# Splitting the chain of small sums behind the keys and values of a linear attention layer

## The reference, cut to what matters

```
q = x @ Wq[i] + bq[i];  k = x @ Wk[i] + bk[i];  v = x @ Wv[i] + bv[i]
Q = elu(q) + 1;  K = elu(k) + 1
KV   = sum over the rows of K * v          # one number for each of 128 columns
Ksum = sum over the rows of K              # the same
Z = 1 / (Q * Ksum + 1e-6)
V = Q * KV * Z
a = gelu(gelu(V @ Wo[i] + bo[i]))
x = layernorm(a + x);  h = gelu(x @ W1[i] + b1[i]);  f = gelu(h @ W2[i] + b2[i]);  x = layernorm(f + x)
```

## Time and profile before

| | us |
|---|---|
| median of three runs | 479.62 |
| the three runs | 478.72, 479.62, 481.2 |
| the profiled execution, its own time | 478.65 |
| its span in the trace | 476.5 |
| outside the span | 2.15 |

### The profile page before, as it was taken

How to read it: one execution, slowest core, us unless ns; L and a number is a source line. 1 busy time by engine, 2 the same in 40 slices (tenths; PEclk the granted TensorE clock), 3 DMA queues, 4 the chain that set the end, 5 groups by cost and what they waited for, 6 DMA issues and landing times.

```text
span 476.5 us, 6527 instructions
## 1 busy us (share of the span) xinstructions
PE 442.0 (93%) x2074; PEld 309.2 (65%) x2074; DVE 402.6 (85%) x1391; ACT 371.9 (78%) x483; POOL 13.9 (3%) x19
## 2 busy tenths in 40 slices
PE   7697999999999999999999999999989999799992
PEld 6465665756575656566656665667566756688992
DVE  5988889995989698969896988698878897978897
ACT  3989877989897989798889888989888717778106
POOL 0000000000000000000000000000000003230000
PEclk9978999999999999999999999999999999999997
DMA  8200000000100000001000000000010102000003
GB/s 285 70 2 0 22 3 0 1 0 1 45 0 2 23 0 1 1 0 45 0 2 1 1 0 1 0 1 2 0 45 12 34 7 82 2 0 23 2 23 132
DMA packets 5360, 10.40 MB, mean 22 GB/s; under 512 B 848, under 2 KB 1872, under 8 KB 5328
## 3 DMA queue, kind: packets, MB, share of 16 engines
q1 hardware_dynamic: 5040, 9.47, 6.1%
q10 hardware_dynamic: 288, 0.52, 0.3%
HBM read 7.90 MB, written 2.10 MB: 21 GB/s over the span
## 4 chain that ended last, share of the span: by engine, by line
PE 41%; DVE 32%; ACT 19%; issue 7%; DMA 1%; ACTq 0%; SPq 0%; DVEq 0%
PE tile L1249 10%; PE tile L1268 7%; PE tile L1226 6%; PE tile L1222 6%; PE tile L1223 5%; DVE stats L770 5%; ACT y L369 3%; DVE y L911 3%; DVE nt L777 2%; ACT y L374 2%; PE tile L1339 2%; PE tile L1328 2%; ACT aa L388 2%; DVE y L880 2%; ACT kq L348 2%
## 5 line engine op out<-in xcount | busy, mean ns | idle before, releaser
L1249 PE MATMUL tile<-h,w 128*128 128x512 f32 x256 | 113.9, 595 | 0.9 <-ACT h L395 0.7
L1222 PE MATMUL tile<-xh,wh 128*128 128x512 f32 x224 | 97.6, 436 | 6.1 <-DVE xh L793 3.4
L1223 PE MATMUL tile<-xh,wl 128*128 128x512 f32 x224 | 89.2, 398 | 0.0
L1249 PEld LDWEIGHTS tile<-h,w 128*128 128x128 f32 x256 | 47.4, 190 | 54.8 <-issue 51.7
L395 ACT ACTIVATE h<-tile,vec 128x1024 f32<-128x1024 f32 x64 | 71.0, 1117 | 13.1 <-PE tile L1226 12.3
L1226 PE MATMUL tile<-xl,wh 128*128 128x512 f32 x224 | 71.1, 398 | 0.7 <-DVE xl L298 0.3
L403 ACT ACTIVATE nt<-tile,work 128x128 f32<-128x128 f32 x140 | 50.7, 482 | 11.3 <-DVE work L739 11.3
L1222 PEld LDWEIGHTS tile<-xh,wh 128*128 128x128 f32 x224 | 42.6, 190 | 24.9 <-DVE xh L793 5.3
L770 DVE BATCH_NORM_STATS2 stats<-tile 128x6 f32<-128x128 f32 x256 | 52.8, 280 | 0.1
L1226 PEld LDWEIGHTS tile<-xl,wh 128*128 128x128 f32 x224 | 41.6, 188 | 13.5 <-DVE xl L799 2.7
L1223 PEld LDWEIGHTS tile<-xh,wl 128*128 128x128 f32 x224 | 42.8, 191 | 9.1 <-issue 2.2
(11 more groups left out here) (173 smaller groups left out, 669.6 us busy)
## 6 DMA issues: line engine op xcount, KB each, us to landing
x<-x_t SPq DMA_DIRECT2D x7, 512.0 KB, 4.1
out_r<-x SPq DMA_DIRECT2D x8, 256.0 KB, 2.0
raw_u<-layers SPq DMA_DIRECT2D x4, 256.0 KB, 3.2
w<-layers SPq DMA_DIRECT2D x4, 256.0 KB, 3.3
raw_a<-layers SPq DMA_DIRECT2D x4, 192.0 KB, 2.8
x<-x_t ACTq DMA_DIRECT2D x2, 256.0 KB, 3.9
wo<-layers SPq DMA_DIRECT2D x4, 64.0 KB, 4.2
fc<-fc_t SPq DMA_DIRECT2D x1, 256.0 KB, 6.5
```

What stands on the lines that cost most here:

```text
L1222: pe.matmul(dst, wh[:, w0:w0 + P], xh[:, part(n, p, at)], start=True, stop=False)
L1223: pe.matmul(dst, wl[:, w0:w0 + P], xh[:, part(n, p, at)], start=False, stop=False)
L1249: mm = pe.matmul(dst, w2[:, (t - 1) // 2 % 2, j * P:(j + 1) * P], h[:, p, j * PAIR + at:j * PAIR + at + BANK], start=(j == 0), stop=(j == ...
```

## The change

`fold_kv` is replaced by six functions. `key_sum`, `key_limits` and `key_inverse` hold the total of the keys, the scale and the limit, and the reciprocal. They are called right behind the step's second keys, which is ahead of values(t, 0) in steps 2 to 7, ahead of both values in step 0 and ahead of queries(1, 1) in step 1. `value_sum`, `value_ratio` and `folded_weights` stay at the place of fold_kv. The scale is now the second increment of `folded` instead of the third, and share_log waits for that.

```
 def share_log(t, p):
-    act.wait_ge(folded, t * FOLD_STEPS + 3)
+    act.wait_ge(folded, t * FOLD_STEPS + 2)
...
-def fold_kv(t):
-    for p in range(2):
-        dve.wait_ge(kv_ready[p], t + 1)
-    dve.wait_ge(wo_in[q], 16 * (t // 4 + 1))
-    dve.tensor_tensor(col[0], ksum[:, 0:1], ksum[:, 1:2], ALU.add).then_inc(folded, 1)
-    dve.tensor_tensor(col[1], kvsum[:, 0:1], kvsum[:, 1:2], ALU.add).then_inc(folded, 1)
...
+def key_sum(t):
+    for p in range(2):
+        dve.wait_ge(k_ready[p], t + 1)
+    dve.tensor_tensor(fold_col(0), ksum[:, 0:1], ksum[:, 1:2], ALU.add).then_inc(folded, 1)
+def key_limits(t):
+    dve.wait_ge(folded, t * FOLD_STEPS + 1)
+    dve.tensor_scalar(fold_col(2), fold_col(0), 1.0 / ZEPS, None, ALU.mult).then_inc(folded, 1)
+    dve.tensor_scalar(fold_col(3), fold_col(0), 2.0 ** -30, None, ALU.max).then_inc(folded, 1)
+def key_inverse(t):
+    dve.wait_ge(folded, t * FOLD_STEPS + 3)
+    dve.reciprocal(fold_col(4), fold_col(3)).then_inc(folded, 1)
+def value_sum(t):
+    for p in range(2):
+        dve.wait_ge(kv_ready[p], t + 1)
+    dve.tensor_tensor(fold_col(1), kvsum[:, 0:1], kvsum[:, 1:2], ALU.add).then_inc(folded, 1)
+def value_ratio(t):
+    dve.wait_ge(folded, t * FOLD_STEPS + 5)
+    dve.tensor_tensor(fold_col(5), fold_col(1), fold_col(4), ALU.mult).then_inc(folded, 1)
+def folded_weights(t):
+    q = t // 2 % 2
+    dve.wait_ge(wo_in[q], 16 * (t // 4 + 1))
+    dve.wait_ge(folded, t * FOLD_STEPS + 6)
+    dve.tensor_scalar(wo_kv[:, :], wo[:, q, :], fold_col(5), -1.0, ALU.mult, ALU.mult).then_inc(folded, 1)
...
     keys(t, 0)
+    key_sum(t)
+    key_limits(t)
+    key_inverse(t)
     values(t, 0)
-    fold_kv(t)
+    value_sum(t)
+    value_ratio(t)
+    folded_weights(t)
     query_round(t, 0)
```

```
 def final_sum(p, u):
     dve.wait_ge(x_cb[p], 1)
+    if n == 0:
+        dve.wait_ge(moment["g"][q], HIDDEN_STEPS)
+    else:
+        dve.wait_ge(moment["x"][q], 3 * MOMENT_STEPS)
```

More of the change, by code:

```diff
@@ L674, in _, with chain @@
         def _(dve):
-            def norm_work(k, t, p, u=None):
-                pair, rows = home(k, t, p), slice(0, ROWS) if u is None else slice(u * HALF, (u + 1) * HALF)
+            def chain(k, t, p):
+                pair = home(k, t, p)
                 if k == "h":
[L680 to L683, removed]
@@ L685, in moments @@
-            def moments(*norms):
[L690 to L764, removed]
@@ new lines, in chain, with sums @@
+                    done, first, at = moment["x"][p], 2 * MOMENT_STEPS, "g"
+                else:
+                    done, first, at = moment[k][p], call_of(k, t) * (HIDDEN_STEPS if k == "g" else MOMENT_STEPS), k
+                return done, first + 3, [value(at, pair, z) for z in range(NCOLS)], {"g": 1, "h": FF}.get(k, P)
+            def sums(k, t, p):
+                done, base, (rstd, shift, m, v, a, b), width = chain(k, t, p)
+                at = home(k, t, p)
+                if k == "g":
+                    for u in range(2):
+                        means = tile[TAIL_SLOTS["p", at, u]][:, :].rearrange("p (b c) -> p b c", c=BANK)[:, :, P:2 * PW:PW]
+                        dve.wait_ge(p_mm[p], 2 * t + u + 1)
+                        dve.tensor_copy(m[:, u * HALF:(u + 1) * HALF].rearrange("p (b c) -> p b c", c=2), means).then_inc(
+                            done, 1)
+                    dve.wait_ge(squared[at], FT)
+                    dve.tensor_scalar(b, squares[:, at, :], 1.0 / FF, OUTER_EPS, ALU.mult, ALU.add).then_inc(done, 1)
+                    return
+                if k == "h":
+                    dve.wait_ge(squared[at], FT)
+                    even, odd, even2, odd2 = (stats_h[:, p, :, c] for c in (1, 4, 2, 5))
+                else:
+                    dve.wait_ge(stats_ready[k][p], call_of(k, t) + 1)
+                    even, odd, even2, odd2 = (stats[k][:, at, :, c] for c in (1, 4, 2, 5))
+                dve.tensor_tensor(a, even, odd, ALU.subtract).then_inc(done, 1)
+                dve.tensor_tensor(b, even2, odd2, ALU.add).then_inc(done, 1)
+                dve.tensor_tensor(m, even, odd, ALU.add).then_inc(done, 1)
@@ new lines, in mean_square, with variance @@
+            def mean_square(k, t, p):
+                done, base, (rstd, shift, m, v, a, b), width = chain(k, t, p)
+                if k == "g":
+                    dve.wait_ge(done, base)
+                    dve.scalar_tensor_tensor(a, m, -1.0, m, ALU.mult, ALU.mult).then_inc(done, 1)
+                else:
+                    dve.wait_ge(done, base - 2)
+                    dve.scalar_tensor_tensor(a, a, width / 4.0, a, ALU.mult, ALU.mult).then_inc(done, 1)
+            def variance(k, t, p):
+                done, base, (rstd, shift, m, v, a, b), width = chain(k, t, p)
+                dve.wait_ge(done, base + 1)
+                if k == "g":
+                    dve.tensor_tensor(v, a, b, ALU.add).then_inc(done, 1)
+                else:
+                    dve.scalar_tensor_tensor(v, b, width * (BLOCK_EPS if k in "12" else OUTER_EPS), a, ALU.add,
+                                             ALU.add).then_inc(done, 1)
@@ new lines, in guess, with guess_squared @@
+            def guess(k, t, p):
+                done, base, (rstd, shift, m, v, a, b), width = chain(k, t, p)
+                dve.wait_ge(done, base + 2)
+                dve.tensor_scalar(b.bitcast(I32), v.bitcast(I32), -0.5, GUESS, ALU.mult, ALU.add).then_inc(done, 1)
+            def guess_squared(k, t, p):
+                done, base, (rstd, shift, m, v, a, b), width = chain(k, t, p)
+                dve.wait_ge(done, base + 3)
+                dve.tensor_tensor(a, b, b, ALU.mult).then_inc(done, 1)
@@ new lines, in row_shift @@
+            def row_shift(k, t, p):
+                done, base, (rstd, shift, m, v, a, b), width = chain(k, t, p)
+                if k != "g":
+                    dve.wait_ge(done, base + 9)
+                    dve.scalar_tensor_tensor(shift, m, -0.5, rstd, ALU.mult, ALU.mult).then_inc(done, 1)
+            def moments(*norms):
+                for level in (sums, mean_square, variance, guess, guess_squared, near_one, quadratics, first_product, root,
+                              row_shift):
+                    for n in norms:
+                        level(*n)
@@ L979, in _ @@
             queries(0, 1)
-            first_low(dve, 2)
+            input_low(2)
             keys(0, 1)
+            key_sum(0)
+            key_limits(0)
+            key_inverse(0)
             values(0, 0)
             values(0, 1)
-            fold_kv(0)
+            value_sum(0)
+            value_ratio(0)
+            folded_weights(0)
             query_round(0, 0)
@@ L998, in _ @@
             keys(1, 1)
+            key_sum(1)
+            key_limits(1)
+            key_inverse(1)
             queries(1, 1)
@@ L1004, in _ @@
             queries(1, 0)
-            fold_kv(1)
+            value_sum(1)
+            value_ratio(1)
+            folded_weights(1)
             row_stats("1", 0, 0)
@@ L1041, in _ @@
             keys(2, 0)
+            key_sum(2)
+            key_limits(2)
+            key_inverse(2)
             values(2, 0)
-            fold_kv(2)
+            value_sum(2)
+            value_ratio(2)
+            folded_weights(2)
             query_round(2, 0)
@@ L1114, in _ @@
             keys(7, 0)
+            key_sum(7)
+            key_limits(7)
+            key_inverse(7)
             values(7, 0)
-            fold_kv(7)
+            value_sum(7)
+            value_ratio(7)
+            folded_weights(7)
             query_round(7, 0)
@@ L1344, in projected, with warm_up @@
                     mm.then_inc(p_mm[p % 2], 1)
-            pe.wait_ge(const_ready, 7)
-            for _ in range(WARM_UP):
-                pe.matmul(tile[3][:, 0:P], ones[:, :], ones[:, :], start=True, stop=True)
+            def warm_up():
+                pe.wait_ge(const_ready, 7)
+                for _ in range(WARM_UP):
+                    pe.matmul(tile[3][:, 0:P], ones[:, :], ones[:, :], start=True, stop=True)
+            warm_up()
             attention_in("k", 0, 0)
```

61 lines of the change are left out of this document (40 added, 21 removed).

## The result

The changed kernel took 480.25 us (median of 20 runs, 478.78 to 481.55), the kernel before 479.1 us (20 runs, 478.49 to 481.2) in the same comparison. The ratio is 1.0022 [1.0011, 1.0032], which is 1.05 us [0.5 to 1.5] more. The forecast was 479.8 us and "no difference that a measurement tells"; the difference is a small loss inside the range. Twenty runs on each side do tell it, though the prediction had put what a measurement tells at 0.5%.

The account below looks back on a forecast made before the run. VectorE's path from the second keys to queries(t, 0) was taken to set ScalarE's time in steps 2 to 7. Six steps at 0.10 us (0.60) plus 0.07 make 0.67 us, from 479.17 to 479.8 us; range 478.5 to 481.3.

Parts of the forecast that it names:

- What bounds the kernel: Steps 2 to 7: the end of queries(t, 0) on VectorE sets ScalarE's time; small sums and values are both on that path.
- The rearrangement, 0.03 us a step: From second keys to query_round: 3.79 us instead of 3.76, with the values starting 0.10 us after the reciprocal.
- The second wait that holds, 0.07 us a step: At the weights, which now wait for Wo and then the ratio: the second wait costs 0.07 us where it holds.
- final_sum, 0.07 us: In final_sum(1, 0) the two waits change places and the second one holds: about 0.09 us instead of 0.02.
- Steps 0 and 1 at nothing: Delays of some 0.2 us (step 0) and about 0.64 us (step 1) vanish in longer waits, so they cost nothing.
- Step 7 at nothing: share_log(7, 1) can start more than 1 us earlier; the 1.44 us become a longer wait at share_log(7, 0), costing nothing.
- The sum: Whole run: 0.60 us for six steps and 0.07 us for final_sum make 0.67 us more, 479.8 us.
- The rule weighed against it: VectorE: only the number of instructions counts and semaphores cost nothing extra, so the time would stay at 479.2 us.
- No change at all: Rival, chance 0.35: second wait hidden under the ratio and reciprocal hidden under the values, 479.2 us.
- Faster: Rival, chance 0.05: the values wait for something of their own, hiding the first part; 3.1 us less, 476.1 us.
- slower: Rival, chance 0.05: fold_out's shift in step 0 keeps TensorE's clock low one more stretch; 2.5 us more, 481.7 us.
- The signs of being wrong: Stretch from second keys to query_round shorter by tenths, ScalarE's wait in steps 2 to 6 ending earlier, or a stretch outside attention moving.

Follow-up runs that it names:

- e5: The changed kernel with the wait for Wo moved from the weights to the total of kvsum (value_sum): 479.14 us, ratio 1.0 to the kernel before.
- e2: The changed kernel with the two waits of the weights, and those of final_sum, in the other order: 479.09 us, 1.0001 of the kernel before.
- e3: The kernel before, chain uncut, with only the wait for Wo moved to the weights, ahead of the wait for the ratio: 479.31 us, 1.0002.
- e1: The changed kernel once more, no edit, for a second profile: 480.57 us, 1.0021 of the kernel before.
- e8: The kernel before once more, no edit, for one more profile: 479.01 us, 0.9998.
- e9: The changed kernel with three more small copies on VectorE in step 0, ahead of first_sum(0, 1): 481.15 us, a single run.
- e10: The changed kernel with ten more small copies on VectorE in step 0, ahead of first_sum(0, 1): 479.54 us, a single run.
- e7: The changed kernel, waits swapped, with value_sum, value_ratio, folded_weights and the reciprocal behind the queries, Wo's wait at value_sum: 476.64 us, 0.9947 of the kernel before.
- e6: The kernel before with ten more small copies on VectorE in step 0, ahead of first_sum(0, 1): 479.11 us, 0.9996.

## Why the prediction was right, step by step

- **What bounds the kernel.** Right. The small sums are on the path in steps 2 to 7, and moving one from behind the values to ahead of them takes nothing off it: e5, with the chain split, has the distance of the kernel before to 0.02 us.
- **The rearrangement, 0.03 us a step.** Too much by 0.02. The values follow the reciprocal after 0.08 us, the low end; 0.10 was taken from the row that reads PSUM. That makes 0.00 to 0.01.
- **The second wait that holds, 0.07 us a step.** Right, and shown from both sides: e2 takes it away, and e3 puts it alone into the old kernel.
- **final_sum, 0.07 us.** Right: 0.03 became 0.11, and 0.03 again in e2.
- **Steps 0 and 1 at nothing.** In the profile the covers were used up as foreseen: first_sum(0, 1) waits 1.06 us instead of 1.37, low 0.22 instead of 0.92, and VectorE 1.76 instead of 1.53 for the transposes. share_log(1, 0) starts at 54.25 us in e1 and 54.39 in the kernel before, but at 55.02 in the first profile of the changed kernel and 52.45 in e8: these steps hold the stretches of lower clock, which shift them by more than the 0.2 us in question. That nothing is lost there rests on the covers.
- **Step 7 at nothing.** Right: the wait of 1.44 us turned into one of 1.99 at the second share_log.
- **The sum.** Forecast 0.67 us. Measured: 6 x 0.08 and 0.08, together 0.56, and the pause of 0.37 in step 4, together 0.93; the medians say 1.05 [0.5 to 1.5]. What the sum lacked is the pause, on which none of its rows had anything; it doesn't reach the edge of the range. The medians hold the lower clock as well, without which 0.3 to 0.8 us are left, so that they lie this close to 0.93 is in part luck.
- **The rule weighed against it** (the Trainium skill, "VectorE: DVE Perf Modes", section "The DRAIN you can't avoid"), by which semaphores between instructions cost nothing extra: e2 and e3 disagree, by 0.07 us for each second wait that holds. The earlier trace rows had a price for this half already: 0.19 to 0.20 us from start to start with one wait between, 0.07 to 0.08 without. The other half the prediction read too strictly: the same section says that a next instruction that is not held starts earlier, so the 0.08 us do not contradict it.
- **The rivals.** "No change at all" is what e2 and e5 became, once the second wait was out of the way; in the change itself that wait cost 0.07 us a step. "Faster" fell: the values waited 0.2 us in all. The clock's stretch in step 0 ("slower") has 0.50 over 3.80 us, against 3.74 before, and did not lengthen by a whole stretch.
- **The signs of being wrong.** Two of them showed in the profile. The stretch of step 4 is not 3.8 to 3.9 us but 4.21, which is the pause. And a stretch outside the attention moved, near 414 us; e8 has the same in the kernel before, so this doesn't speak against the sum.

**What stays open** is the pause's cause. It is shown that it repeats at its place (e1), that it moves or hides when instructions are added far ahead (e9, e10), and that the split chain doesn't bring it to the weights (e9, e10). In all five traces where one is seen on VectorE, a packet of the queue for instructions (q14) follows it, 0.64 to 0.67 us after the held instruction started: at 199.2 us in the changed kernel, 198.4 in e1, 198.1 in e2, 242.9 in e7 and 151.7 in e10. The nine traces without a pause in step 4 have such a packet there too, between 195.4 and 201.4 us, and 0.66 us before it VectorE was inside an instruction of 0.69 us or 1.28 us, under which a pause can't be seen (e5, e6 and e9: the values).

ScalarE has a pause of this kind in all twelve traces. In step 1 the load of a function table (L379) starts 0.33 to 0.35 us behind the wait ahead of it, where in step 0 it is 0.03, and a packet of q14 follows 0.64 to 0.91 us after that start. The kernel before, from the chain that ended last:

```profile
58.80 0.02 ACTq L378
58.82 0.33 issue
59.15 1.28 ACT L379
```

This suggests that an engine waited for its next block of instructions. But the row of a packet doesn't say which engine it was for, and no run takes the packets away. It is an argument and not shown. The row of the changed kernel's DMA view, window 199.1 to 199.2 us:

```profile
q14 instruction: 1, 0.01, 21.4%
```

## What to carry to other kernels

Before splitting a chain on the engine that sets the path, ask whether the piece that moves leaves the path: ahead of the same full instruction it doesn't, behind the last one that the next engine waits for it does, and here that alone was worth 0.6%, until TensorE took over. Where an instruction needs two waits, write the one that will hold first and hang the one long satisfied on an instruction that has a second wait already. And read a difference of a few tenths of a microsecond at a distance between two fixed events in the trace, within stretches of equal clock; the run times here could not tell 0.4 us.

## What was unexpected in the hardware

VectorE can be held for 0.19 to 0.37 us by nothing that the profile shows, at a place that repeats from run to run and goes elsewhere or out of sight when three or ten instructions are added far ahead. ScalarE has 0.33 to 0.35 us of the same at one place in all twelve traces. And the same kernel, twice profiled, had TensorE's granted clock at 1.00 from 410 to 416 us once and at 0.50 in two of these microseconds the other time.
